# Layer-0 rows of a softmax graph network, turned by VectorE's 32x32 block transpose instead of TensorE

## The chip, the cores and the metric

One core of a Trainium2 chip runs the whole program. The metric is the device time of one execution in microseconds. The engines are TensorE (PE; its weight loads are PEld), VectorE (DVE), ScalarE (ACT) and GpSimd (POOL); SyncE (SP) issues the DMAs. Each engine runs its own list of instructions in order and meets the others at semaphores only.

## The reference

128 graphs of 64 nodes with 384 features pass through two graph networks, each followed by a residual sum and a normalisation. The change lies in the second network, two layers of this:

```python
u = jnp.einsum('bid,bjd->bij', h, h) / temper
a = jax.nn.softmax(u, axis=-1)
delta = a * adjacency_matrix
attn = delta / (jnp.sum(delta, axis=-1, keepdims=True) + 1e-10)
hl = h @ wl.T + b_l;  hs = h @ ws.T + b_s;  hr = h @ wr.T + b_r
ctx = einsum(attn * upper, hl) + diag_a[..., None] * hs + einsum(attn * lower, hr)
o = (ctx - mean) / jnp.sqrt(var + LN_EPS) * g + beta      # then relu
```

All is in float32. `h` is x1, the output of the first network, in layer 0, and the output of layer 0 in layer 1.

## The kernel before

**Tiles and units.** A unit is one layer of 512 tokens (8 graphs, `NT` = 4 tiles of 128 tokens). Two streams of 512 tokens are worked on at a time, so a pass has four units: 0 and 1 are layer 0 of stream 0 and 1, units 2 and 3 are layer 1 of them. Eight passes cover the 8192 tokens. The first network (`gated_layers`, L108 to L916) runs its eight passes first and writes x1 to DRAM; then `softmax_layers` (L919 on) runs the second. All engines' orders are written out by hand.

**High and low halves.** A float32 product is made as three products of rounded operands (`three_products`): hi x hi, hi x lo, lo x hi. ScalarE writes the high half with a copy to float32r, VectorE or GpSimd subtracts it from the full value for the low half.

**What a unit does.** Its input must lie feature-major: `ht_hi` and `ht_lo`, [128 features, 3 blocks k, 512 tokens]. In the unit before, `turn_block` (L1090) waits for the input and turns block k with four 128x128 TensorE transposes (L1104) into one of two PSUM banks `turn`; `turn_out` (L1195) on ScalarE copies the bank to `ht_hi` (L1201 in layer 0; in layer 1, L1204, gain, shift and relu as well), and `turn_lo` (L1413) on VectorE subtracts `ht_hi` from the bank into `ht_lo` (L1416). In layer 0 the input is `x_in`, rows of x1, in layer 1 it is `z`. The same banks hold the masked exponentials (`raw`, `side_prob`) until the low halves of the probabilities are made (L1454), so the first two blocks wait for `prob_lo_ready`, the third for the low half of the first.

Then come, on TensorE: `scores` (L1111, in the unit before, behind the last value), `fold_parts`, twelve `values` (L1134: 4 tiles x 3 weight matrices, nine matmuls each, into a ring of four PSUM banks) and four `contexts` (L1146: four tiles, into the same ring; tile t waits for `v_lo_ready`). VectorE empties the ring: `biased_value` (L1437) for a value, `contexts_out` (L1471) and statistics (L1474) for a context tile. ScalarE makes `v_hi` (L1238), GpSimd `v_lo` (L1329). Units of layer 1 are followed, inside the next unit, by gain and shift on GpSimd (L1353, L1355), by the residual on VectorE (L1514), by the final statistics (L1520), variance, root (L1348) and offset (L1533), and by the final normalise on ScalarE (L1244), which stands ahead of the exponentials of the unit after. So units 3 and 0 carry this extra work, and units 1 and 2 don't.

**Order around the turn (VectorE, `up_to_contexts`).** Values 3, 4, 5; probabilities; value 6; low probabilities; value 7; value 8; low halves 0 and 1; value 9; low half 2; value 10; own probability; residual (0, 1); value 11; residual (2, 3) and final statistics; contexts out; final offset. On TensorE blocks 0 and 1 are turned behind value 8 and block 2 behind value 9.

**Loads.** `load_x` (L1037) reads 512 rows of x1, row p of a tile to partition p, in pieces of 1536 bytes; SP then copies `x_in` to `x_res` for the residual (L1059), and loads `x_in` anew when the copy has landed and the blocks are turned. The very first unit of the second network is turned inside the first (`next_turn`, L393).

## Time and profile before

| | |
|---|---|
| median of 3 runs | 1760.14 us (1759.49 to 1760.24) |
| the profiled execution | 1760.6 us, span of its instructions 1758.8 us |
| TensorE matmuls | 1695.9 us busy (96% of the span), 9856 |
| VectorE | 1255.1 us (71%), 2735 |
| ScalarE | 882.7 us (50%), 1785 |
| GpSimd | 825.3 us (47%), 860 |
| second network | from about 846 us on; a pass takes 108.8 us |
| units 3, 0, 1, 2 of pass 3 and 4 | from 1275.8, 1302.7, 1330.4, 1357.3 |

A row of a timeline gives the start in us from the first instruction, the length in us of the merged run, the engine, the line of the kernel, the operation, output<-inputs with their shapes, how many instructions were merged, and in brackets the idle time of the engine before it and what ended it. Two instructions of one engine overlap by some 0.1 us in it, since the next begins while the last drains: from start to start a row of two takes less than twice one. The third number from the end of a window is the granted share of TensorE's 2.4 GHz.

### The profile page before, as it was taken

How to read it: one execution, taken by the hardware profiler on the slowest of the kernel's cores; microseconds unless marked ns; L12 is line 12 of the kernel's file. 1: busy time of each engine (PE TensorE's matmuls, PEld its weight loads, DVE VectorE, ACT ScalarE, POOL GpSimd, SP SyncE). 2: the span in 40 equal slices, each digit the busy share in tenths (PEclk: the TensorE clock that was granted, in tenths of full speed). 3: DMA queues.
4: the chain of work that ended last, by engine and by line, in shares of the span. 5: the costliest groups of instructions: out<-in, count | busy, mean ns of one | idle time of the engine just before them, and what ended most of it. 6: DMA issues, size and time to landing. Idle time of an engine off the chain costs nothing.

```text
span 1758.8 us, 30529 instructions
## 1 busy us (share of the span) xinstructions
PE 1695.9 (96%) x9856; PEld 1601.9 (91%) x9856; DVE 1255.1 (71%) x2735; ACT 882.7 (50%) x1785; POOL 825.3 (47%) x860
## 2 busy tenths in 40 slices
PE   7999999999999999999889999999999999999994
PEld 6989989898998988998789999999999999999994
DVE  4587685958768586786846867768677686776766
ACT  4545455464545546455445464454554545544542
POOL 5143242424324243334546646666465664656635
PEclk9999999999999999999899999999999999999997
DMA  7014030020202102030111020201202011020200
GB/s 224 1 31 153 6 104 15 24 89 28 91 6 64 55 24 89 6 114 17 49 50 58 21 92 21 92 0 34 80 21 92 0 54 59 21 92 0 75 1 36
DMA packets 76358, 91.98 MB, mean 52 GB/s; under 512 B 29600, under 2 KB 67488, under 8 KB 76320
## 3 DMA queue, kind: packets, MB, share of 16 engines
q1 hardware_dynamic: 76320, 91.51, 15.7%
q8 instruction: 20, 0.33, 0.1%
q14 instruction: 18, 0.15, 0.0%
HBM read 53.75 MB, written 25.17 MB: 45 GB/s over the span
## 4 chain that ended last, share of the span: by engine, by line
PE 38%; issue 36%; POOL 16%; DVE 4%; ACT 3%; SPq 1%; DMA 1%; POOLq 0%; DVEq 0%; ACTq 0%
PE b_work L1143 24%; PE b_work L1155 5%; POOL g_qv_lo L620 3%; POOL b_ht L600 3%; POOL s_v_lo L1329 3%; PE b_work L355 2%; PE b_turn L1104 2%; PE b_score_ps L105 2%; POOL b_z L1353 1%; PE b_work L379 1%; PE b_score_ps L369 1%; POOL g_keep_l L615 1%; POOL b_z L1355 1%; POOL g_sigma L629 1%; POOL g_a_nat L616 1%
## 5 line engine op out<-in xcount | busy, mean ns | idle before, releaser
L1143 PE MATMUL b_work<-b_w_hi,b_ht 128*128 128x384 f32 x2304 | 615.7, 340 | 0.0
L1143 PEld LDWEIGHTS b_work<-b_w_hi,b_ht 128*128 128x128 f32 x2304 | 420.9, 189 | 0.0
L1143 PE MATMUL b_work<-b_w_lo,b_ht 128*128 128x384 f32 x1152 | 387.4, 336 | 0.0
L355 PE MATMUL b_work<-b_ht,b_w_hi 128*128 128x512 f32 x1152 | 357.7, 392 | 9.8 <-DVE b_w_lo L695 9.8
L1329 POOL TENSOR_TENSOR s_v_lo<-s_v_full,s_v_hi 128x384 fp32r<-128x384 f32 x256 | 247.4, 983 | 198.2 <-ACT s_v_hi L1238 197.4
L620 POOL TENSOR_TENSOR g_qv_lo<-g_v_full,g_qv_hi 128x384 fp32r<-128x384 f32 x128 | 133.2, 1060 | 360.5 <-ACT g_qv_hi L493 360.5
L355 PEld LDWEIGHTS b_work<-b_ht,b_w_hi 128*128 128x128 f32 x1152 | 216.2, 189 | 51.2 <-issue 9.7
L355 PE MATMUL b_work<-b_ht,b_w_lo 128*128 128x512 f32 x576 | 225.9, 392 | 0.0
L1143 PEld LDWEIGHTS b_work<-b_w_lo,b_ht 128*128 128x128 f32 x1152 | 218.1, 189 | 0.0
L718 DVE TENSOR_TENSOR g_qv_lo<-b_work,g_qv_hi 128x512 fp32r<-128x512 f32 x192 | 128.7, 687 | 111.9 <-ACT g_qv_hi L481 110.0
L379 PE MATMUL b_work<-b_w_hi,b_ht 128*128 128x384 f32 x768 | 206.5, 336 | 0.0
L1437 DVE TENSOR_TENSOR s_v_full<-b_work,b_bias 128x384 f32<-128x384 f32 x256 | 140.3, 553 | 81.6 <-PE b_work L1143 81.6
L481 ACT ACTIVATE g_qv_hi<-b_work 128x512 fp32r<-128x512 f32 x192 | 110.6, 591 | 132.2 <-PE b_work L355 132.1
L1238 ACT ACTIVATE s_v_hi<-s_v_full 128x384 fp32r<-128x384 f32 x256 | 129.4, 529 | 86.1 <-DVE s_v_full L1437 86.1
L369 PE MATMUL b_score_ps<-g_qv_hi,b_ht 128*128 128x256 f32 x768 | 146.9, 285 | 4.8 <-DVE g_qv_lo L718 4.8
L379 PEld LDWEIGHTS b_work<-b_w_hi,b_ht 128*128 128x128 f32 x768 | 139.9, 188 | 1.3
L355 PEld LDWEIGHTS b_work<-b_ht,b_w_lo 128*128 128x128 f32 x576 | 108.7, 189 | 23.0
L379 PE MATMUL b_work<-b_w_lo,b_ht 128*128 128x384 f32 x384 | 128.8, 335 | 0.0
L369 PEld LDWEIGHTS b_score_ps<-g_qv_hi,b_ht 128*128 128x128 f32 x768 | 120.6, 188 | 8.5 <-DVE g_qv_lo L718 7.4
L1437 DVE TENSOR_TENSOR s_v_own<-b_work,b_bias 128x384 f32<-128x384 f32 x128 | 71.1, 555 | 65.3 <-PE b_work L1143 64.9
L369 PE MATMUL b_score_ps<-g_qv_lo,b_ht 128*128 128x256 f32 x384 | 107.3, 279 | 0.0
L1244 ACT ACTIVATE b_z<-b_z,s_foffset,s_frstd 128x384 f32<-128x384 f32 x62 | 39.0, 699 | 134.8 <-DVE s_foffset L1533 134.8
(138 smaller groups left out, 3225.0 us busy)
## 6 DMA issues: line engine op xcount, KB each, us to landing
b_x_in<-in_x_t SPq DMA_DIRECT2D x16, 768.0 KB, 7.0
g_x_res<-in_x SPq DMA_DIRECT2D x16, 768.0 KB, 7.7
x<-b_z SPq DMA_DIRECT2D x16, 768.0 KB, 3.9
b_x_in<-x SPq DMA_DIRECT2D x16, 768.0 KB, 5.1
s_x_res<-b_x_in SPq DMA_DIRECT2D x16, 768.0 KB, 5.4
out<-b_z SPq DMA_DIRECT2D x15, 768.0 KB, 3.6
b_a_tr<-in_adj_t SPq DMA_DIRECT2D x64, 64.0 KB, 3.4
g_a_nat<-in_adj SPq DMA_DIRECT2D x32, 64.0 KB, 2.5
```

What stands on the lines that cost most here:

```text
L355: mm = pe.matmul(bank[:], w, h, start=(n == 0), stop=(n == len(pairs) - 1))
L369: mm = pe.matmul(score_ps[:, t, :, :], h, q, start=(n == 0), stop=(n == len(pairs) - 1))
L379: mm = pe.matmul(bank[:, 0:H], h, w, start=(n == 0), stop=(n == len(pairs) - 1))
L481: nc.scalar.activation(q_hi[:, m, :, d, :], work[use % RING][:], ACT.Copy).then_inc(q_hi_ready, 1)
L600: nc.gpsimd.tensor_tensor(ht_lo[s][:, k, :], xt_in[s][:, k, :], ht_hi[s][:, k, :].bitcast(F32), ALU.subtract).then_inc(x_split, 1)
L620: nc.gpsimd.tensor_tensor(v_lo[:, t, 0:H], v_full[:, t, :], v_hi[:, t, 0:H].bitcast(F32), ALU.subtract).then_inc(v_lo_ready, 1)
L718: op = nc.vector.tensor_tensor(q_lo[:, m, :, d, :], bank, q_hi[:, m, :, d, :].bitcast(F32), ALU.subtract)
L1143: mm = pe.matmul(bank[:, 0:H], h, w, start=(n == 0), stop=(n == len(pairs) - 1))
L1155: mm = pe.matmul(bank[:, 0:HC], p, v, start=(n == 0), stop=(n == len(pairs) - 1))
L1238: nc.scalar.activation(v_hi[:, t, n, 0:H], v_full[:, (2 * t + n) % VF, :], ACT.Copy)\
L1329: nc.gpsimd.tensor_tensor(v_lo[:, t, n, 0:H], v_full[:, (2 * t + n) % VF, :], v_hi[:, t, n, 0:H].bitcast(F32), ALU.subtract).then_inc(v_lo ...
L1437: nc.vector.tensor_tensor(dst, work[(unit * WN + j) % RING][:, 0:H], bias[:, side, layer, :], ALU.add).then_inc(work_free, 1)
```

## The change

Layer-0 rows of the second network are no longer turned by TensorE, except for the very first unit.

- `load_x` reads x1 in four DMAs, one for each quarter of 32 partitions. Partition q*32+t of block b (16 blocks of 32 tokens) holds token b*32+t, features q*96 to q*96+95: pieces of 384 bytes.
- `flip_block` on VectorE turns block k with one instruction over [128, 16 x 32]: 32 features of every third column, 32x32 blocks, into `turned_x`, a new SBUF buffer of two slots [128, 2, 512]. It waits for the load, and for k = 2 for the low half of block 0. Row p of block k is now feature 3p + k, so the layer-0 weights are loaded in that order too, and `next_turn` reads every third column.
- `turn_out` and `turn_lo` of layer 0 read `turned_x` in place of the PSUM bank.
- Order: on VectorE the flips 0 and 1 stand behind values 3 and 4, ahead of the probabilities; low half 0 and flip 2 behind value 7; low half 1 behind value 8; low half 2 behind value 9. On ScalarE blocks 0 and 1 stand ahead of `values_hi(2)`.
- `x_res` is read from x1 in DRAM, no longer copied from `x_in`, and SP no longer waits for that copy.

```diff
             def load_x(i, s):
-                sp.dma_start(x_in[s][:], x_v[i, s]).then_inc(x_loaded[s], 16)
+                for q in range(QUADS):
+                    sp.dma_start(sh.x_blocks[s][quarter(q)], x_b[i, s, q]).then_inc(x_loaded[s], 16)
...
-                    sp.wait_ge(x_loaded[s], 16 * (i + 1))
-
                     wait(sp, summed, i * (STREAMS * NT) + (s + 1 - STREAMS) * NT)
-                    sp.dma_start(x_res[s][:], x_in[s][:]).then_inc(x_copied[s], 16)
+                    sp.dma_start(x_res[s][:], x_v[i, s]).then_inc(x_copied[s], 16)
                     if not last:
                         sp.wait_ge(turned, nth(i, s, KO, KO - 1))
-                        sp.wait_ge(x_copied[s], 16 * (i + 1))
                         load_x(i + 1, s)
...
+                    turn_next = more and layer_of(unit + 1) == 1
...
-                    if more:
+                    if turn_next:
                         turn_block(i, unit + 1, 0)
                         turn_block(i, unit + 1, 1)
...
                 if layer == 0:
-                    nc.scalar.activation(ht_hi[s][:, k, :], bank[:], ACT.Copy).then_inc(turn_read, 1)
+                    nc.scalar.activation(ht_hi[s][:, k, :], turned_x[:, k % XK, :], ACT.Copy).then_inc(turn_read, 1)
...
+                flip_next = more and layer_of(unit + 1) == 0
+                if flip_next:
+                    turn_out(i, unit + 1, 0)
+                    turn_out(i, unit + 1, 1)
                 values_hi(i, unit, 2)
...
             def turn_lo(i, unit, k):
                 s = unit % STREAMS
+                full = turned_x[:, k % XK, :] if layer_of(unit) == 0 else turn[(unit * KO + k) % 2][:]
                 dve.wait_ge(turn_read, nth(i, unit, KO, k))
-                nc.vector.tensor_tensor(ht_lo[s][:, k, :], turn[(unit * KO + k) % 2][:],
-                                        ht_hi[s][:, k, :].bitcast(F32), ALU.subtract).then_inc(ht_ready, 1)
+                nc.vector.tensor_tensor(ht_lo[s][:, k, :], full, ht_hi[s][:, k, :].bitcast(F32),
+                                        ALU.subtract).then_inc(ht_ready, 1)
+
+            def flip_block(i, unit, k):
+                s = unit % STREAMS
+                dve.wait_ge(x_loaded[s], x_parts(i, unit))
+                if k >= XK:
+                    dve.wait_ge(ht_ready, nth(i, unit, KO, k - XK))
+                blocks = sh.x_blocks[s][:, :, k:KO * QUAD:KO]
+                nc.vector.transpose(turned_x[:, k % XK, :].rearrange("p (b t) -> p b t", b=TOK // QUAD), blocks)\
+                    .then_inc(turned, 1)
...
                 for j in range(3, 6):
                     biased_value(i, unit, j)
+                    if flip_next and j - 3 < XK:
+                        flip_block(i, unit + 1, j - 3)
                 probabilities(i, unit)
                 biased_value(i, unit, 6)
                 probabilities_lo(i, unit)
                 biased_value(i, unit, 7)
+                if flip_next:
+                    turn_lo(i, unit + 1, 0)
+                    flip_block(i, unit + 1, 2)
                 biased_value(i, unit, 8)
                 if more:
-                    turn_lo(i, unit + 1, 0)
+                    turn_lo(i, unit + 1, 1 if flip_next else 0)
+                if turn_next:
                     turn_lo(i, unit + 1, 1)
```

At the start of the second network the written-out order gets the same: flips 0, 1, 2 behind values 3, 4, 5, low half 0 behind value 5, low half 1 behind value 7, low half 2 behind value 9 as before.


## Rows read from the trace of the kernel before

**Rows 1.** Waits, second network: who waited for whom, us, times, longest.

```profile
PE b_turn L1104 <- DVE b_ht L1416: 16.8, 17, 7.1
...
PE b_work L1155 <- POOL s_v_lo L1329: 5.5, 7, 0.8
```

**Rows 2.** Timeline of TensorE, unit 0: start, us, engine, line, op [idle before <-releaser].

```profile
1317.46 1.04 PE L1104 MATMUL b_turn<-b_const,b_x_in 128*128 128x128 f32 x8
...
1323.51 1.59 PE L105 MATMUL b_score_ps<-b_ht 128*128 128x256 f32 x12
...
1329.26 0.44 PE L1155 MATMUL b_work<-s_v_hi,s_prob_hi 128*128 128x386 f32 x1 [0.79 <-POOL s_v_lo L1329]
```

**Rows 3.** Timeline of VectorE, unit 0, a value at TensorE's pace.

```profile
1311.41 0.56 DVE L1437 TENSOR_TENSOR s_v_full<-b_work,b_bias 128x384 f32<-128x384 f32 x1 [1.00 <-PE b_work L1143]
```

**Rows 4.** Timelines of ScalarE (first two) and GpSimd, unit 0.

```profile
1306.98 2.51 ACT L1244 ACTIVATE b_z<-b_z,s_foffset,s_frstd 128x384 f32<-128x384 f32 x4 [7.55 <-DVE s_foffset L1533]
...
1311.01 0.96 ACT L1238 ACTIVATE s_v_hi<-s_v_full 128x384 fp32r<-128x384 f32 x2
...
1311.64 1.85 POOL L1329 TENSOR_TENSOR s_v_lo<-s_v_full,s_v_hi 128x384 fp32r<-128x384 f32 x2 [2.80 <-ACT s_v_hi L1238]
...
1324.54 4.59 POOL L1329 TENSOR_TENSOR s_v_lo<-s_v_full,s_v_hi 128x384 fp32r<-128x384 f32 x4
```

**Rows 5.** Timeline of VectorE, unit 3 and the start of unit 0.

```profile
1289.87 0.55 DVE L1437 TENSOR_TENSOR s_v_full<-b_work,b_bias 128x384 f32<-128x384 f32 x1
...
1293.76 0.56 DVE L1437 TENSOR_TENSOR s_v_full<-b_work,b_bias 128x384 f32<-128x384 f32 x1 [0.18 <-PE b_work L1143]
...
1294.74 0.69 DVE L1416 TENSOR_TENSOR b_ht<-b_turn,b_ht 128x512 fp32r<-128x512 f32 x1 [0.42 <-ACT b_ht L1201]
...
1295.76 0.56 DVE L1437 TENSOR_TENSOR s_v_full<-b_work,b_bias 128x384 f32<-128x384 f32 x1 [0.33 <-PE b_work L1143]
...
1296.83 1.70 DVE L1514 SCALAR_TENSOR_TENSOR b_z<-b_z,s_x_res 128x384 f32<-128x384 f32 x2
...
1306.80 0.15 DVE L1533 SCALAR_TENSOR_TENSOR s_foffset<-s_fmv,s_frstd 128x4 f32<-128x4 f32 x1
```

**Rows 6.** One line's instructions (duration ns min/median/max): reduce from SBUF; L1416.

```profile
L1459 DVE TENSOR_REDUCE s_own<-s_expo x32: 674/676/678, 879.1 to 1730.1; 128x4 f32<-128x512 f32 x32
...
L1416 DVE TENSOR_TENSOR b_ht<-b_turn,b_ht x93: 676/692/694, 873.8 to 1703.9; 128x512 fp32r<-128x512 f32 x93
```

**Rows 7.** L706's instructions; timelines of VectorE beside GpSimd; GpSimd alone (last row).

```profile
L706 DVE TENSOR_TENSOR b_ht<-g_ht_full,b_ht x48: 691/693/1336, 53.8 to 811.9; 128x512 fp32r<-128x512 f32 x48
...
809.26 1.16 DVE L706 TENSOR_TENSOR b_ht<-g_ht_full,b_ht 128x512 fp32r<-128x512 f32 x1 [2.76 <-ACT b_ht L473]
...
810.81 2.46 DVE L706 TENSOR_TENSOR b_ht<-g_ht_full,b_ht 128x512 fp32r<-128x512 f32 x2
...
806.91 7.24 POOL L606 TENSOR_TENSOR b_w_lo<-g_next_stage,b_w_hi 128x384 fp32r<-128x384 f32 x6 [9.09 <-ACT b_w_hi L456]
...
900.35 5.82 POOL L1313 TENSOR_TENSOR b_w_lo<-s_x_res,b_w_hi 128x384 fp32r<-128x384 f32 x6 [2.34 <-ACT b_w_hi L1193]
```

**Rows 8.** Timeline of GpSimd, unit 3.

```profile
1293.55 2.81 POOL L1329 TENSOR_TENSOR s_v_lo<-s_v_full,s_v_hi 128x384 fp32r<-128x384 f32 x3
```

**Rows 9.** Windows: stretch, busy of each engine, granted clock, DMA share, GB/s.

```profile
843.60:845.90 2.30, 0.00 (x1) 0.01 (x1) 1.23 (x4) 1.01 (x2) 2.05 (x3) 1.00 0.13 29
...
846.30:849.70 3.40, 3.40 (x16) 3.40 (x16) 0.93 (x3) 0.93 (x3) 2.98 (x3) 0.50 0.00 0
```

**Rows 10.** Timelines at the start: TensorE (first two), VectorE.

```profile
874.58 1.11 PE L1104 MATMUL b_turn<-b_const,b_x_in 128*128 128x128 f32 x4 [6.17 <-DVE b_ht L1416]
...
880.89 1.59 PE L105 MATMUL b_score_ps<-b_ht 128*128 128x256 f32 x12
...
876.36 0.69 DVE L1416 TENSOR_TENSOR b_ht<-b_turn,b_ht 128x512 fp32r<-128x512 f32 x1 [0.27 <-ACT b_ht L1201]
```

**Rows 11.** SP's loads of x rows: issue ns min/median/max.

```profile
L1038 SPq DMA_DIRECT2D b_x_in<-x x14: 363/398/403, 924.0 to 1567.8; - x14
```

More of the change, by code:

```diff
@@ L21 @@
 BIG = 1e30
+QUAD = 32
+QUADS = P // QUAD
 C_EYE, C_LE, C_GT, C_LT = 0, 128, 256, 384
@@ L69, in __init__ @@
         self.x_in = [sb(f"x_in{s}", [P, NT, H]) for s in range(STREAMS)]
+        self.x_blocks = [b[:].rearrange("p t h -> p (t h)").rearrange("p (b f) -> p b f", b=TOK // QUAD)
+                         for b in self.x_in]
         self.a_tr = [sb(f"a_tr{s}", [P, NT, P]) for s in range(STREAMS)]
@@ L91, in __init__, with quarter @@
         self.adj_loaded = [ctx.enter_context(nc.semaphore(f"b_adj_loaded{s}")) for s in range(STREAMS)]
+def quarter(q):
+    return slice(q * QUAD, (q + 1) * QUAD)
 def three_products(H_hi, H_lo, W_hi, W_lo):
@@ L280, in one_pass @@
                         sp.wait_ge(stored[s], 16 * 2)
-                        sp.dma_start(x_in[s][:], x1_v[0, s]).then_inc(sh.x_loaded[s], 16)
+                        if s == 0:
+                            sp.dma_start(x_in[s][:], x1_v[0, s]).then_inc(sh.x_loaded[s], 16)
+                        else:
+                            for q in range(QUADS):
+                                sp.dma_start(sh.x_blocks[s][quarter(q)], x1_b[0, s, q]).then_inc(sh.x_loaded[s], 16)
                 for s in range(STREAMS):
@@ L298, in next_weights @@
             def next_weights(n):
[L299 removed]
+                sp.dma_start(next_stage[n % 2][:], next_w[n][0].rearrange("(p k) o -> p k o", p=P))\
                     .then_inc(next_stage_in[n], 16)
@@ L400, in next_turn @@
                 for t in range(NT):
-                    mm = pe.transpose(turn[k % 2][:, t * P:(t + 1) * P], x_in[0][:, t, k * P:(k + 1) * P], eye)
+                    mm = pe.transpose(turn[k % 2][:, t * P:(t + 1) * P], x_in[0][:, t, k:H:KO], eye)
                 mm.then_inc(sh.turned, 1)
@@ L935, in softmax_layers @@
     LAST_GT = 1
+    XK = 2
     VF = 4
@@ L959, in softmax_layers @@
         expo = sb("expo", [P, NT, P])
+        turned_x = sb("turned_x", [P, XK, TOK])
         prob_hi = [sb(f"prob_hi{n}", [P, NT, P], F32R) for n in range(2)]
@@ L1020, in layer_of, with x_parts @@
             return unit % UNITS // STREAMS
+        def x_parts(i, unit):
+            s = unit % STREAMS
+            return 16 * QUADS * (i + unit // UNITS + s) + 16 * (1 - s)
         def in_layer(i, unit):
@@ L1037, in load_x @@
             def load_x(i, s):
-                sp.dma_start(x_in[s][:], x_v[i, s]).then_inc(x_loaded[s], 16)
+                for q in range(QUADS):
+                    sp.dma_start(sh.x_blocks[s][quarter(q)], x_b[i, s, q]).then_inc(x_loaded[s], 16)
             def load_adj(i, s):
@@ L1090, in turn_block @@
             def turn_block(i, unit, k):
-                layer, s = divmod(unit % UNITS, STREAMS)
-                src = x_in[s] if layer == 0 else z[s]
-                if layer == 0:
-                    pe.wait_ge(x_loaded[s], i * 16 + 16 * (unit // UNITS + 1))
-                else:
-                    pe.wait_ge(z_ready, i * (STREAMS * NT) + NT * (s + 1))
+                s = unit % STREAMS
+                pe.wait_ge(z_ready, i * (STREAMS * NT) + NT * (s + 1))
                 if k < 2:
@@ L1103, in turn_block @@
                 for t in range(NT):
-                    mm = pe.transpose(bank[:, t * P:(t + 1) * P], src[:, t, k * P:(k + 1) * P], eye)
+                    mm = pe.transpose(bank[:, t * P:(t + 1) * P], z[s][:, t, k * P:(k + 1) * P], eye)
                 mm.then_inc(turned, 1)
@@ L1171, in one_pass @@
                     values(i, unit, 9)
-                    if more:
+                    if turn_next:
                         turn_block(i, unit + 1, 2)
@@ L1268, in second_half @@
                 if more:
-                    for k in range(KO):
+                    for k in range(2 if flip_next else 0, KO):
                         turn_out(i, unit + 1, k)
@@ L1293, in _ @@
             gated_normalise(0)
-            for t in range(3):
-                values_hi(0, 0, t)
-            for k in range(KO):
-                turn_out(0, 1, k)
+            values_hi(0, 0, 0)
+            values_hi(0, 0, 1)
+            turn_out(0, 1, 0)
+            turn_out(0, 1, 1)
+            turn_out(0, 1, 2)
+            values_hi(0, 0, 2)
             values_hi(0, 0, 3)
@@ L1545, in up_to_contexts @@
                 more = not (last and unit == UNITS - 1)
+                flip_next = more and layer_of(unit + 1) == 0
+                turn_next = more and layer_of(unit + 1) == 1
                 for j in range(3, 6):
                     biased_value(i, unit, j)
+                    if flip_next and j - 3 < XK:
+                        flip_block(i, unit + 1, j - 3)
                 probabilities(i, unit)
@@ L1605, in _ @@
             biased_value(0, 0, 3)
+            flip_block(0, 1, 0)
             gated.gain_and_shift(2)
             biased_value(0, 0, 4)
+            flip_block(0, 1, 1)
             gated.gain_and_shift(3)
             biased_value(0, 0, 5)
+            turn_lo(0, 1, 0)
+            flip_block(0, 1, 2)
             gated.residual_and_stats((0, 1))
@@ L1612, in _ @@
             biased_value(0, 0, 7)
+            turn_lo(0, 1, 1)
             gated.residual_and_stats((2, 3))
             biased_value(0, 0, 8)
-            turn_lo(0, 1, 0)
-            turn_lo(0, 1, 1)
             gated.final_var()
```

5 lines of the change are left out of this document (4 added, 1 removed).

## The prediction

> **What bounds the kernel now.** I read the page first: TensorE is busy 96% of the span, VectorE 71%, GpSimd 47%. So 12 transposes less per layer-0 unit ought to be time won, and the question is where something else ends last. The waits of the second network answer it [rows 1]: TensorE waits for VectorE's low halves at the third transpose, mostly in two start-up stalls, and 7 times, 0.8 us each, for GpSimd's low halves of the values (L1329). That second wait stands once per pass, in unit 0, and unit 0 comes right after unit 3. These are the two units that turn the layer-0 rows of a next unit. Units 1 and 2 turn z, which the change leaves alone; there TensorE runs through.
>
> Then the timeline of these two units. TensorE's first transpose in unit 0 is at 1317.46 and the scores at 1323.51 [rows 2]; the 27 matmuls between take 3 x 1.56 us (one value per 0.56 busy and 1.00 idle on VectorE [rows 3]), so 12 transposes cost 6.05 - 4.68 = 1.37 us. In the same rows the last context tile starts at 1329.26, after 0.79 us of idle TensorE. What comes before it is a chain through four engines [rows 4]: the final offset on VectorE (1306.80), ScalarE's final normalise that waited 7.55 us for it and behind which the exponentials and the first v_hi stand, GpSimd's first v_lo at 1311.64, which waited 2.80 us for that v_hi, and then GpSimd without a pause until the four v_lo from 1324.54 have ended at 1329.13. The offset in turn ends an unbroken run of VectorE that begins with the value of 1295.76 in unit 3 [rows 5], which waited 0.33 us for TensorE. So unit 0 ends when this chain lets it, and only the part of the gain that moves the chain's start counts there.
>
> **TensorE.** 15 units lose 1.37 us of transposes: 7 times in unit 3, 7 times in unit 0, once at the start. Taken alone, 20.6 us. In unit 0 this is covered by the wait for GpSimd, which is there already: 7 x 1.37 us worth nothing, unless GpSimd's chain gets shorter. What is left to win is unit 3's share, if it arrives at 1295.76.
>
> **VectorE in unit 3.** Added: three flips. The trace has no block transpose; the nearest row is the reduce over 128x512 from SBUF, 0.68 us, or 0.59 from start to start [rows 6]. I take 0.60; bounds 0.5 and 1.3 (twice the reduce). The first two stand behind values 3 and 4, where VectorE idles a microsecond or more per value, and are hidden. The third lies in the tight stretch. The three low halves (L1416) move from bank + SBUF to two SBUF inputs, turned_x and ht_hi. The same subtraction with two SBUF inputs is L706: 693 ns in the median, but 1.16 and 2 x 1.23 us in the three that run beside GpSimd's L606 [rows 7], so 1.16 us from start to start against 0.61. In unit 3 GpSimd is at work in this stretch too [rows 8]. After value 7 VectorE is free at 1290.34: low half 1.16, flip 0.60, value 8 0.47, low half 1.16, value 9 0.47, low half 1.16 give 1295.36 for value 10, against 1295.76 now [rows 5]. Of TensorE's 1.37 us some 0.4 arrive. The residual adds of 1296.83, also with two SBUF inputs, then run beside a GpSimd that is later, for which I take off 0.2. The chain starts 0.2 us earlier. Bounds: 1.37 earlier (no contention), 0.6 later (slow flip). TensorE's scores wait for the third low half at 1295.4 and are not due before 1295.9: hidden.
>
> **GpSimd in unit 0.** Six subtractions of one form take 5.82 us alone and 7.24 us beside those three low halves [rows 7]: (7.24 - 5.82) / 3 = 0.47 us lost to GpSimd per contended low half. In unit 0 the three low halves fall on the unbroken run of rows 4: 3 x 0.47 = 1.4 us later at its end. Bounds 0.9 (0.3 each) and 2.1 (each holds GpSimd for its 0.69). With one SBUF input, as L1416 has now, they cost nothing: its 93 stay within 676 to 694 ns. The Trainium skill has a rule for this, in "SBUF — State Buffer", section "SBUF: two separate sides": VectorE with two SBUF inputs and GpSimd exclude each other for a whole instruction. Rows 7 agree in kind; by the rule the loss would be the upper bound, an estimate of 5 us more in all.
>
> Sum for a pass: 1.4 - 0.2 = 1.2 us later, times 7 = 8.4 us.
>
> **The clock.** TensorE now comes to the wait of unit 0 earlier by 2 x 1.37 us less some 0.6 (value 0 of unit 0 must wait for its bank, freed by a VectorE that didn't gain). The third context tile needs v_lo from the middle of the last GpSimd group, some 1.2 us later than now, so 2.1 + 1.2 = 3.3 us open up in front of it, less what VectorE's late low halves take of it at the scores: 2.5 to 3.3 us of idle, and about 1 us more stands in front of the fourth. When TensorE was idle for 2.35 us at 843.5 (0.00 busy in that window), 3.4 us at a granted clock of 0.50 followed [rows 9], that is the lower level, 1.2 GHz. 3.4 us at half speed cost 1.7, less 0.3 that fall on the idle: 1.4. The idle is about as long as the one row that I have, so I count half of the passes: 7 x 0.5 x 1.4 = 4.9 us.
>
> **The start.** TensorE's stall of 6.17 us before 874.58 and the half speed behind it go; what is late next is the third low half, which the scores wait for. It starts at 876.36 and would be 3 flips (1.8) and up to 1.5 us of contention later, so it ends between 878.8 and 880.3, against scores at 880.89 [rows 10]. A gain of 0.5 to 2; I take 1.5. The other start-up stall (7.1 us [rows 1]) stands in unit 1, which turns z, and stays.
>
> **What costs nothing.** Four loads for one on SP's queue, 0.40 us of issue each [rows 11], and pieces of 384 B for 1536: issued two units (some 50 us) before their use, where even four times the present 5.0 us to land is hidden; behind them on SP stand only adjacency loads and output stores. x_res is read from DRAM at the same point of the queue, and SP loses two waits. ScalarE turns blocks 0 and 1 ahead of values_hi(2): 1.2 us later for GpSimd, which is behind anyway in these units. The flips' own waits hold nobody: the rows have long landed, and the third follows on VectorE right behind the low half that it waits for. The strided read of 12 transposes at the start is 3 us of TensorE at most beside a VectorE that bounds.
>
> **Sum**, on the profiled execution (1760.6 us; span 1758.8 and 1.8 around it; 0.03% above the median of 1760.14): 1760.6 + 8.4 + 4.9 - 1.5 = 1772 us.
>
> **Rivals.**
> 1. *The low halves do not collide.* They could fall between GpSimd's instructions. Then value 10 starts 1.37 us earlier, GpSimd's chain too, and no long idle appears: 1760.6 - 7 x 1.37 - 2 = 1749 us. Against it: both engines are busy without pause there, and all three L706 beside L606 were hit. Chance 0.18.
> 2. *Break-even.* 0.9 us lost on GpSimd, 0.9 won at value 10, no clock loss: 1759 us. Chance 0.17.
> 3. *A slow flip.* The source is read at a stride of 12 bytes. At 1.3 us each the third flip delays value 10 by 0.7 in each of 7 passes, and the start by up to 2: about 1778 us. No row speaks for it or against. The Trainium skill, "Advanced Engine Details and Errata", section "SBUF Cachelines", wants at least two accesses per 16-byte line, which this stride gives only every third time; no run here shows it. Chance 0.13.
> 4. *The loads come too late*, so that flips wait: excluded by the 50 us, 0.02.
>
> The forecast itself, the collision in unit 0 outweighing unit 3's gain: 0.50. It turns into a gain where the loss on GpSimd falls under what reaches value 10. Slower side: with the clock falling in every pass and 2.1 us on GpSimd, 1782. Range 1754 to 1784; it leaves out most of rival 1. A measurement can tell about 0.2% (3.5 us) from no change. Faster takes rival 1 and a part of 2: 0.22; same the rest of 2: 0.15; slower 0.63.
>
> **What would show it.** Right: L1104 left with the transposes of z alone; the low halves at 1.0 to 1.3 us instead of 0.69 in units 3 and 0; GpSimd's unbroken run in unit 0 longer by 1.4 us than 17.5; TensorE's wait for v_lo at 3 us and more per pass, and stretches at 0.50 clock near it; flips at 0.6. Wrong: low halves at 0.69, or TensorE without a wait in unit 0, or passes of the second network that get shorter.

## The result and the profile after

The changed kernel takes 1772.57 us in the median of 4 runs (1772.5 to 1772.76), the kernel before on the same chip 1760.19 us (1759.49 to 1760.44): the ratio is 1.0071, with a 95% interval of 1.0054 to 1.0089. It is slower by 12.4 us. The profiled execution took 1772.5 us, its span is 1770.7 us against 1758.8.

In the changed kernel the lines have other numbers: values L1159, contexts L1171, the fold that opens a unit L1136, the scores L114, the low halves L1440, the flips L1450, the residual adds L1548, the context tiles on VectorE L1505, GpSimd's v_lo L1352, gain and shift L1376 and L1378.

Waits of TensorE after the change (us in total, times, longest), the answer to [rows 1]:

```profile
PE b_work L1171 <- POOL s_v_lo L1352: 16.0, 14, 1.5
PE b_turn L1120 <- DVE b_ht L1440: 10.8, 16, 7.2
...
PE b_score_ps L114 <- DVE b_ht L1440: 6.6, 8, 0.9
PE b_work L1159 <- DVE b_z L1505: 5.4, 7, 0.8
...
PE b_work L1159 <- DVE s_v_full L1471: 3.7, 2, 2.8
...
PE b_work L1159 <- DVE s_v_own L1471: 2.1, 1, 2.1
```

One start-up stall has gone. The wait for GpSimd's low halves has grown from 5.5 us in 7 to 16.0 us in 14, and four kinds of wait are new. Where they stand shows TensorE's timeline of one unit 0 (start, us, op [idle before <- releaser]), the answer to [rows 2]:

```profile
1307.81 0.40 PE L1136 MATMUL b_score_ps<-b_part,b_eye_r 128*128 128x256 f32 x2
...
1309.38 0.44 PE L1159 MATMUL b_work<-b_w_hi,b_ht 128*128 128x384 f32 x1 [0.78 <-DVE b_z L1505]
...
1329.22 1.69 PE L114 MATMUL b_score_ps<-b_ht 128*128 128x256 f32 x12 [0.85 <-DVE b_ht L1440]
...
1334.56 0.44 PE L1171 MATMUL b_work<-s_v_hi,s_prob_hi 128*128 128x386 f32 x1 [1.53 <-POOL s_v_lo L1352]
1336.66 0.44 PE L1171 MATMUL b_work<-s_v_hi,s_prob_hi 128*128 128x386 f32 x1 [0.80 <-POOL s_v_lo L1352]
1337.83 0.40 PE L1136 MATMUL b_score_ps<-b_part,b_eye_r 128*128 128x256 f32 x2
```

Four waits, 3.96 us, between the fold of unit 0 and that of unit 1. A unit is measured here from fold to fold: this one is 1337.83 - 1307.81 = 30.02 us long. The same subtraction gives, in us, for a pass in which the clock stays up:

| kernel | unit 2 | unit 3 | unit 0 | unit 1 | a pass |
|---|---|---|---|---|---|
| before | 27.35 | 26.88 | 27.71 | 26.86 | 108.8 |
| after | 27.35 | 25.56 | 30.02 | 26.88 | 109.8 |

Unit 3 gained 1.32 us, unit 0 lost 2.31. Times 7 that is 6.9 us. In 2 of the 7 passes the granted clock fell behind these waits as well, and units 0 and 1 were together 1.6 us longer than in the others: 3.2 us. Up to unit 2 of the first pass 2.0 us were lost. The sum is 12.1 us, against 11.9 us of span.

VectorE and GpSimd in the same unit 0 (VectorE's three low halves; GpSimd from the start to the end of its run, answering [rows 4]):

```profile
1323.74 1.49 DVE L1440 TENSOR_TENSOR b_ht<-s_turned_x,b_ht 128x512 fp32r<-128x512 f32 x1
...
1326.56 1.19 DVE L1440 TENSOR_TENSOR b_ht<-s_turned_x,b_ht 128x512 fp32r<-128x512 f32 x1
...
1328.14 1.03 DVE L1440 TENSOR_TENSOR b_ht<-s_turned_x,b_ht 128x512 fp32r<-128x512 f32 x1
```

```profile
1318.01 1.85 POOL L1352 TENSOR_TENSOR s_v_lo<-s_v_full,s_v_hi 128x384 fp32r<-128x384 f32 x2 [2.91 <-ACT s_v_hi L1255]
...
1323.66 2.29 POOL L1352 TENSOR_TENSOR s_v_lo<-s_v_full,s_v_hi 128x384 fp32r<-128x384 f32 x2
1325.91 1.29 POOL L1363 TENSOR_TENSOR s_expo<-s_expo,s_keep 128x512 f32<-128x512 f32 x1
1327.17 1.46 POOL L1376 TENSOR_TENSOR b_z<-b_z,b_gain 128x384 f32<-128x384 f32 x1
1328.70 1.34 POOL L1378 TENSOR_TENSOR b_z<-b_z,b_shift 128x384 f32<-128x384 f32 x1
...
1331.97 4.56 POOL L1352 TENSOR_TENSOR s_v_lo<-s_v_full,s_v_hi 128x384 fp32r<-128x384 f32 x4
```

Each low half lengthens the GpSimd operation that comes next: 2.29 us against the 1.85 of the same pair at 1318.01, 1.46 and 1.34 against 1.02 each for gain and shift left alone. And the low halves are long themselves, in a way that shows what happens. The second one ends at 1326.56 + 1.19 = 1327.75, and the GpSimd operation that was at work when it began ended at 1325.91 + 1.29 = 1327.20, 0.55 us earlier. That distance is 0.55 us in all 43 low halves that began beside a GpSimd operation, whether 0.33 or 0.94 us of that operation were left. The GpSimd operation behind it ends 0.72 or 0.87 us after the low half (42 of the 43; such an operation takes 0.87 or 1.02 us alone). So the two engines take turns, operation by operation: VectorE waits for the end of GpSimd's, and GpSimd's next then waits for VectorE, all but its first 0.15 us. The two kinds of L1440 in the whole run, and the flips (duration ns min/median/max):

```profile
L1440 DVE TENSOR_TENSOR b_ht<-b_turn,b_ht x48: 690/691/694, 911.3 to 1715.8; 128x512 fp32r<-128x512 f32 x48
L1440 DVE TENSOR_TENSOR b_ht<-s_turned_x,b_ht x45: 675/998/1486, 869.4 to 1659.1; 128x512 fp32r<-128x512 f32 x45
...
L1450 DVE STREAM_TRANSPOSE s_turned_x<-b_x_in x45: 851/877/895, 862.3 to 1656.2; 128x512 f32<-128x512 f32 x45
```

One line, one shape, one output; the one operand that comes from the PSUM bank instead of SBUF goes with the difference between 694 and 1486 ns at most. The 48 from the bank stand in other units, where GpSimd works less beside them; but in the kernel before, 28 of the 93 low halves [rows 6] had GpSimd at work for over nine tenths of their length, and took 680 to 692 ns. The flips stay within 44 ns of each other, whatever GpSimd does.

### The profile page after: what moved, and what is told of

It reads as the page before. It is cut to its first block, busy times and chain, and to the rows that moved or that the text cites. A ratio compares the mean times of both kernels' runs of the same rounds, so it can differ in the third digit from the quotient of the medians.

```text
span 1770.7 us, 30284 instructions
## 1 busy us (share of the span) xinstructions
PE 1685.3 (95%) x9676; PEld 1587.0 (90%) x9676; DVE 1313.4 (74%) x2780; ACT 884.0 (50%) x1785; POOL 842.4 (48%) x860
## 4 chain that ended last, share of the span: by engine, by line
issue 44%; POOL 24%; PE 21%; DVE 6%; ACT 3%; SPq 1%; DMA 1%; POOLq 1%; DVEq 0%; ACTq 0%
PE b_work L1159 11%; POOL s_v_lo L1352 6%; POOL g_qv_lo L634 3%; POOL b_ht L614 3%; POOL b_z L1376 2%; PE b_work L1171 2%; PE b_work L369 2%; POOL b_z L1378 2%; PE b_work L393 1%; PE b_score_ps L383 1%; POOL s_expo L1363 1%; POOL s_keep L1346 1%; POOL g_keep_l L629 1%; POOL g_sigma L643 1%; POOL g_a_nat L630 1%
## 5 line engine op out<-in xcount | busy, mean ns | idle before, releaser
L1159 PE MATMUL b_work<-b_w_hi,b_ht 128*128 128x384 f32 x2304 | 610.6, 340 | 11.2 <-DVE b_z L1505 5.4
L1159 PEld LDWEIGHTS b_work<-b_w_hi,b_ht 128*128 128x128 f32 x2304 | 421.7, 190 | 13.3 <-DVE b_z L1505 6.4
L1159 PE MATMUL b_work<-b_w_lo,b_ht 128*128 128x384 f32 x1152 | 387.7, 337 | 0.0
L1352 POOL TENSOR_TENSOR s_v_lo<-s_v_full,s_v_hi 128x384 fp32r<-128x384 f32 x256 | 255.5, 1015 | 200.9 <-ACT s_v_hi L1255 199.9
L1159 PEld LDWEIGHTS b_work<-b_w_lo,b_ht 128*128 128x128 f32 x1152 | 218.6, 190 | 0.0
```

The costliest lines, as they stand in the source:

```text
L1159: mm = pe.matmul(bank[:, 0:H], h, w, start=(n == 0), stop=(n == len(pairs) - 1))
L1352: nc.gpsimd.tensor_tensor(v_lo[:, t, n, 0:H], v_full[:, (2 * t + n) % VF, :], v_hi[:, t, n, 0:H].bitcast(F32), ALU.subtract).then_inc(v_lo ...
```

## The experiments

Twelve kernels, each against the kernel before on the same chip. All of them are about three questions: is it the collision, why does the saved TensorE time not arrive without it, and what holds the units then.

### 1. The collision and the flips, each alone

The changed kernel, low halves from the bank:

```diff
-                full = turned_x[:, k % XK, :] if layer_of(unit) == 0 else turn[(unit * KO + k) % 2][:]
+                full = turn[(unit * KO + k) % 2][:]
...
-                                        ALU.subtract).then_inc(ht_ready, 1)
+                                        ALU.is_equal if layer_of(unit) == 0 else ALU.subtract).then_inc(ht_ready, 1)
```

> The changed kernel, but the low halves of layer 0 take their first input from the PSUM bank again instead of turned_x (and compare instead of subtracting, so that the numbers stay small: ht_lo of layer 0 is then no low half, and the output is another). Flips, loads, orders stay as changed. Theory (two SBUF inputs collide with GpSimd): low halves at 0.69 us; GpSimd's unbroken run in unit 0 back from 18.5 to 17.5 us; the run starts 1.0 to 1.4 us earlier after the start of unit 3 than before the change; a pass is 1.2 to 1.4 us shorter than before, so 1751 to 1753 us. Rival (the flips, of 0.88 us each, or the new orders are what costs): no more than 2 us below the changed kernel's 1772.6.

Measured: 1760.95 us, ratio 1.0004 (0.9994 to 1.0014). The 12 us are back, but no more than that: the 1751 to 1753 us expected are missed by 8.

The kernel before, low halves of layer 0 from SBUF (a buffer that is set to zero once):

```diff
+                full = turned_x[:, k % 2, :] if layer_of(unit) == 0 else turn[(unit * KO + k) % 2][:]
...
-                nc.vector.tensor_tensor(ht_lo[s][:, k, :], turn[(unit * KO + k) % 2][:],
+                nc.vector.tensor_tensor(ht_lo[s][:, k, :], full,
```

> The kernel before, transposes on TensorE and all, with one edit: the low halves of layer 0 read a buffer of zeros in SBUF in place of the PSUM bank (ht_lo is then no low half, and the output is another). Theory: low halves at 0.9 to 1.5 us, GpSimd's run in unit 0 1.0 to 1.4 us longer, TensorE's wait for v_lo as much longer, 7 passes: 1767 to 1770 us. Rival (SBUF input is harmless there, the flips or the loads cost): 1760 to 1761 us.

Measured: 1775.97 us, ratio 1.0096 (1.0079 to 1.0112): more than the whole loss and 6 us above the range expected, with TensorE's transposes still in place and no flip anywhere. Its unit 0 is 29.4 us, and in one pass the clock falls as well. Its low halves of layer 0 (L1419 here) lengthened as in the change:

```profile
L1419 DVE TENSOR_TENSOR b_ht<-s_turned_x,b_ht x45: 678/1039/1773, 874.7 to 1660.7; 128x512 fp32r<-128x512 f32 x45
```

The kernel before with flips into a buffer that nobody reads, behind values 3, 4 and 7. There are 42 of them and not the 45 of the expectation, since the start of the second network has none:

```diff
                 for j in range(3, 6):
                     biased_value(i, unit, j)
+                    if flip_next and j < 5:
+                        flip_block(i, unit + 1, j - 3)
...
                 biased_value(i, unit, 7)
+                if flip_next:
+                    flip_block(i, unit + 1, 2)
```

> The kernel before, with 45 block transposes added on VectorE at the places of the change, into a buffer that nobody reads; TensorE still turns. The source is read in the old layout, at the same stride of 12 bytes. Theory: a flip has one SBUF input and doesn't hold GpSimd; the first two fit where VectorE waits for TensorE, the third into 2.2 us of idle time in unit 3: 1760 to 1763 us, the start of the second network taking what there is. Rival (a slow flip is the cause): 1766 us or more.

Measured: 1760.28 us, ratio 1.0 (0.9991 to 1.001). The flips of the passes fall into VectorE's idle time; those at the start were not tested alone.

So the loss is the collision. It was shown both ways: put in alone it costs 16 us, taken out it gives 12 back. The kernel that gives them back has the new loads and orders too, so these are not what costs. A form of the change that keeps all its work and reads the bank: ScalarE copies the turned block a second time, into the bank, and its copies and the low halves stand in the order of before.

```diff
-                    nc.scalar.activation(ht_hi[s][:, k, :], turned_x[:, k % XK, :], ACT.Copy).then_inc(turn_read, 1)
+                    nc.scalar.activation(ht_hi[s][:, k, :], turned_x[:, k % XK, :], ACT.Copy)
...
+                    nc.scalar.activation(bank[:], turned_x[:, k % XK, :], ACT.Copy).then_inc(turn_read, 1)
```

> A repair: ScalarE copies each turned block from turned_x to ht_hi and then also into the PSUM bank, once the bank is free, and the low half reads the bank, in the order of before (halves 0 and 1 behind value 8, half 2 behind value 9); flip 2 stands behind low half 0. Three more ScalarE copies of 0.6 us for each layer-0 unit, at a place where ScalarE idles. Theory: no contention, TensorE's saving in unit 3 reaches GpSimd's run: 1751 to 1754 us, faster than both. Rival: ScalarE's second copy makes the low halves late, TensorE waits at the scores, and the time is between 1756 and 1765.

Measured: 1764.87 us, ratio 1.0025 (1.0015 to 1.0034). Better than the change by 7.7 us, but not the 1751 to 1754 expected. It lies in the range of its rival, and the rival is right in part: TensorE waits 0.48 us at the scores of unit 0. But it also waits 0.52 and 1.11 us for v_lo there. Both kernels without the collision miss their expectation by about 10 us, so something else stands in unit 0.

### 2. Why the saving does not arrive: GpSimd's run

TensorE in a unit 0 of the first kernel above (low halves from the bank):

```profile
1435.39 0.44 PE L1171 MATMUL b_work<-s_v_hi,s_prob_hi 128*128 128x386 f32 x1 [1.73 <-POOL s_v_lo L1352]
1437.19 0.44 PE L1171 MATMUL b_work<-s_v_hi,s_prob_hi 128*128 128x386 f32 x1 [0.47 <-POOL s_v_lo L1352]
```

Units 3 and 0 are 25.55 and 28.3 us, together 53.85 against 54.59 before: of 2 x 1.37 us saved 0.74 arrive. The rest has turned into the wait for v_lo. And the clock takes back what arrives. In four of the seven passes it stays up, and a pass is 108.1 us, 0.7 less than before. In the other three it falls to half for 3.4 to 6.8 us, which makes them 1.5 to 2.9 us longer, 6.0 us in all, more than the 7 x 0.74 = 5.2 us that arrive; the kernel before has no such stretch in a pass. So this kernel is level with the kernel before, and not some 5 us faster, because of the clock.

GpSimd's run, from its first v_lo to its last in unit 0, starts 35.26 us after unit 3's start here and 35.83 before. VectorE explains why the start is only 0.57 us earlier; value 10 and the adds behind it, in unit 3 of this kernel:

```profile
1403.10 0.56 DVE L1471 TENSOR_TENSOR s_v_full<-b_work,b_bias 128x384 f32<-128x384 f32 x1 [0.33 <-PE b_work L1159]
...
1404.16 2.49 DVE L1548 SCALAR_TENSOR_TENSOR b_z<-b_z,s_x_res 128x384 f32<-128x384 f32 x2
```

Value 10 is 1.3 us earlier (18.61 us into the unit against 19.95), but the residual adds, two SBUF operands as well, now meet GpSimd's v_lo and take 2.49 us against 1.70 [rows 5].

Two experiments on that run. First, the changed kernel with GpSimd's last gain and shift of a pass over 8 columns:

```diff
+                w = 8 if s == 1 and t == 3 else H
...
-                nc.gpsimd.tensor_tensor(z[s][:, t, 0:H], z[s][:, t, 0:H], gain[:], ALU.mult).then_inc(gained, 1)
+                nc.gpsimd.tensor_tensor(z[s][:, t, 0:w], z[s][:, t, 0:w], gain[:, 0:w], ALU.mult).then_inc(gained, 1)
...
```

> The changed kernel, with GpSimd's last gain and shift of each pass (unit 3, tile 3, 0.86 and 1.06 us) over 8 columns instead of 384, so the output isn't the reference's there: GpSimd's run is some 1.7 us shorter and nothing else is changed. Theory (GpSimd's run ends unit 0): 1.5 to 1.8 us less a pass and the clock drops with it, 1758 us (1756 to 1762). Rival (VectorE's lengthened low halves end it, and GpSimd only seems to be waited for): over 1769 us.

Measured: 1759.61 us, ratio 0.9997 (0.9987 to 1.0006): 13 us less than the changed kernel, for 1.24 us less work on GpSimd in a pass. The two operations of that run:

```profile
1325.34 0.19 POOL L1377 TENSOR_TENSOR b_z<-b_z,b_gain 128x8 f32<-128x8 f32 x1
1325.62 0.49 POOL L1379 TENSOR_TENSOR b_z<-b_z,b_shift 128x8 f32<-128x8 f32 x1
```

0.68 us against 0.86 + 1.06 in the changed kernel. Unit 0 is 28.82 us, 1.2 less, and no half-clock stretch is left in the passes. GpSimd's run ends unit 0; with the collision untouched, shortening it pays one for one: 7 x 1.2 us and the 3.2 us of the clock are 11.6 of the 13.

Second, an order that starts the run earlier. ScalarE idles 7.55 us ahead of block 0's last normalising [rows 4]; that goes behind the normalise of unit 3:

```diff
                     normalise(i, unit, more)
+                    if unit == UNITS - 1 and not last:
+                        final_normalise(i, 0)
...
-                    if unit >= STREAMS:
+                    if unit == UNITS - 1 or last and unit == STREAMS:
                         final_normalise(i, unit - STREAMS, tiles=NT if more else NT // 2)
```

On the kernel before:

> The kernel before, with one thing moved: in unit 3 ScalarE's normalising of the finished block 0 (2.5 us, which waits for VectorE's offset) goes from ahead of unit 0's exponentials and v_hi 0 to behind the normalise. All work is done. Theory (GpSimd's run of 17.5 us, which v_hi 0 releases 35.8 us after unit 3's start, is what ends unit 0, and ScalarE stands idle for 7.5 us ahead of it): the run starts some 2.8 us earlier, TensorE's wait of 0.8 us for v_lo in each of 7 passes goes, 1754.5 us (1753 to 1756). Rival (that wait is something else's, or GpSimd's earlier halves collide with VectorE and give it back): 1760 us.

On the changed kernel:

> The changed kernel with the same one thing moved (block 0's normalising on ScalarE goes behind unit 3's normalise). The low halves still read two SBUF operands beside GpSimd. Theory (the collisions cost time only because they lengthen GpSimd's run and VectorE's chain, which end unit 0): unit 0 falls from 30.0 us to about 27.2 us (25.5 of TensorE's own work and the waits of 0.78 and 0.85 us for a value bank and a low half), 1750 us (1748 to 1754). Rival (VectorE's collisions hold TensorE by themselves): under 5 us gained, above 1767 us.

On the variant with the copies into the bank:

> The kernel in which ScalarE also copies the turned block into the PSUM bank and the low half reads the bank (1764.9 us), with the same normalising moved. Theory: its unit 0 waits 0.5 and 1.1 us for GpSimd's low halves, both go, unit 0 falls from 28.5 to about 26.9 us, its unit 1 of 27.8 us stays: 1753 us (1751 to 1756). Rival: no better than 1763 us.

Measured, in this order: 1759.78 us (ratio 0.9996, 0.9987 to 1.0005), 1768.65 us (1.0046, 1.003 to 1.0061) and 1757.6 us (0.9984, 0.9975 to 0.9993). The first two miss and fall on the rival's side, the third is 1.6 us above its range. The run does start earlier. The wait for GpSimd is gone from unit 0 in the first and third kernel and down to 0.46 us in the second. But the time comes back in unit 1 (passes in which the clock stays up):

| kernel | unit 3 | unit 0 | unit 1 | a pass |
|---|---|---|---|---|
| before | 26.88 | 27.71 | 26.86 | 108.8 |
| before, reordered | 26.88 | 26.60 | 27.85 | 108.7 |
| after | 25.56 | 30.02 | 26.88 | 109.8 |
| after, reordered | 25.55 | 27.82 | 28.91 | 109.6 |
| low halves from the bank | 25.55 | 28.31 | 26.88 | 108.1 |
| copies into the bank | 25.55 | 28.54 | 27.81 | 109.3 |
| the same, reordered | 25.55 | 26.77 | 28.44 | 108.1 |

### 3. The second chain: VectorE

Rows of the reordered kernel before: GpSimd's run (its first and last group), TensorE at the start of unit 1, and VectorE ahead of it.

```profile
1308.87 1.85 POOL L1331 TENSOR_TENSOR s_v_lo<-s_v_full,s_v_hi 128x384 fp32r<-128x384 f32 x2
...
1322.22 4.27 POOL L1331 TENSOR_TENSOR s_v_lo<-s_v_full,s_v_hi 128x384 fp32r<-128x384 f32 x4
```

```profile
1329.29 0.40 PE L1120 MATMUL b_score_ps<-b_part,b_eye_r 128*128 128x256 f32 x2
1330.61 0.44 PE L1143 MATMUL b_work<-b_w_hi,b_ht 128*128 128x384 f32 x1 [0.52 <-DVE b_z L1473]
```

```profile
1322.34 0.56 DVE L1439 TENSOR_TENSOR s_v_full<-b_work,b_bias 128x384 f32<-128x384 f32 x1 [0.34 <-PE b_work L1143]
...
1323.41 2.35 DVE L1516 SCALAR_TENSOR_TENSOR b_z<-b_z,s_x_res 128x384 f32<-128x384 f32 x2
...
1326.15 1.22 DVE L1516 SCALAR_TENSOR_TENSOR b_z<-b_z,s_x_res 128x384 f32<-128x384 f32 x2
1327.29 1.93 DVE L1522 BATCH_NORM_STATS2 s_fstats<-b_z 128x6 f32<-128x384 f32 x4
...
1329.94 0.62 DVE L1473 SCALAR_TENSOR_TENSOR b_z<-s_v_own,s_own,b_work 128x385 f32<-128x385 f32 x1
```

GpSimd's run starts at 1308.87 instead of 1311.64 and ends at 1326.49 instead of 1329.13 (the two unit 3 start within 0.01 us of each other). VectorE gains nothing from it: from value 10, at TensorE's pace, over the adds and the final statistics to the first context tile it is busy without a pause for 8 us, and that tile is taken out of its bank at 1329.94. Value 0 of unit 1 needs the bank. In the kernel before the same tile is taken out at nearly the same time (VectorE), and value 0 of unit 1 (TensorE) finds its bank free:

```profile
1330.00 0.62 DVE L1471 SCALAR_TENSOR_TENSOR b_z<-s_v_own,s_own,b_work 128x385 f32<-128x385 f32 x1
```

```profile
1331.06 0.39 PE L1143 MATMUL b_work<-b_w_hi,b_ht 128*128 128x384 f32 x1
```

The bank is free at 1330.00 + 0.62 = 1330.62. So TensorE came only 0.44 us too late to wait for this chain; where it comes earlier, because the wait for GpSimd is gone, the chain holds it.

I tried to take the second by order too: the first two context tiles ahead of the final statistics, GpSimd's masks ahead of its final root.

```diff
                     add_residual(i, s, (2, 3))
+                    contexts_out(i, unit, (0, 1))
                     final_stats(i, s)
                     final_var(i, s)
-                contexts_out(i, unit)
-                if s is not None:
+                    contexts_out(i, unit, (2, 3))
                     final_offset(i, s)
+                else:
+                    contexts_out(i, unit)
```

On the reordered variant with the copies, on the reordered kernel before, and on the kernel with low halves from the bank, in this order:

> The bank variant with the normalising moved (1757.6 us), and VectorE's own chain shortened too: in units 3 and 0 the first two context tiles are taken out of their banks ahead of the final statistics (2.5 us) instead of behind them, and GpSimd's masks go ahead of its final root. All work is done. Theory (two chains end units 0 and 1: GpSimd's run, and VectorE's from value 10 over the residual adds and the statistics to the context tiles whose banks value 0 of the next unit takes): TensorE's waits of 0.4 and 1.1 us for those banks go, the wait of 0.8 for a low half stays; 1747.5 us (1745 to 1751). Rival (VectorE only shifts its work, and the later tiles or the next unit's values are late in their place): 1755 us or more.

> The kernel before with both moves (the normalising on ScalarE, the context tiles on VectorE and the masks on GpSimd), no block transposes. With the first alone unit 0 was 1.1 us shorter and unit 1 1.0 us longer (1759.8 us). Theory: that unit 1's wait of 0.5 us and what goes with it is VectorE's chain, and goes now: unit 1 back at 26.86, 1.1 us less a pass, 1752.5 us (1751 to 1755). Rival (it is something else's): 1759 us or more.

> The changed kernel, its low halves reading the PSUM bank (a compare with whatever is in it, so the low half of layer 0 is left out), and both moves. It shows what taking the transposes off TensorE is worth once neither chain holds the units. Theory: units 0 and 3 are TensorE's own 25.5 us each, 105.3 us a pass against 108.8: 24 us less, 1736 us (1734 to 1741). Rival (something else holds unit 0 above 26.5 us): 1744 us or more.

Measured: 1763.59 us (ratio 1.002, 1.0011 to 1.0029), 1765.42 us (1.003, 1.0019 to 1.0041) and 1752.03 us (0.9953, 0.9939 to 0.9967). All three came out on the rival's side, the third 16 us above its expectation. VectorE and TensorE in the second of them:

```profile
1328.12 2.31 DVE L1516 SCALAR_TENSOR_TENSOR b_z<-b_z,s_x_res 128x384 f32<-128x384 f32 x2
1330.36 0.60 DVE L1473 SCALAR_TENSOR_TENSOR b_z<-s_v_own,s_own,b_work 128x385 f32<-128x385 f32 x1
...
1335.13 0.62 DVE L1473 SCALAR_TENSOR_TENSOR b_z<-s_v_own,s_own,b_work 128x385 f32<-128x385 f32 x1
```

```profile
1331.27 0.40 PE L1120 MATMUL b_score_ps<-b_part,b_eye_r 128*128 128x256 f32 x2
1335.80 0.44 PE L1143 MATMUL b_work<-b_w_hi,b_ht 128*128 128x384 f32 x1 [0.55 <-DVE b_z L1473]
```

The wait has moved from the first bank to the third, whose tile stands behind the statistics now, and the masks, moved forward, meet the second pair of adds (2.31 us against 1.22). In all three kernels TensorE now waits another 0.7 us in unit 1, for the low probabilities. Unit 1 became 28.6 to 29.3 us in the three. This order only shifted a chain in which VectorE never idles. So the last kernel leaves work out: low halves from the bank, ScalarE's order moved, context tiles in their old place, the final statistics over 8 columns.

```diff
-                    nc.vector.bn_stats(fstats[:, t, :], z[s][:, t, 0:H]).then_inc(fstats_ready, 1)
+                    nc.vector.bn_stats(fstats[:, t, :], z[s][:, t, 0:8]).then_inc(fstats_ready, 1)
```

> The changed kernel with its low halves reading the PSUM bank (layer 0's low half left out), the normalising of block 0 moved on ScalarE, the context tiles in their old place, and VectorE's final statistics over 8 columns instead of 384 (so the last normalisation's mean and variance are of 8 columns): both chains shortened, one by order and one by leaving 1.4 us of work out. Theory (GpSimd's run and VectorE's chain from value 10 to the context tiles are what keeps TensorE's saving from arriving): unit 0 about 25.8 us and unit 1 26.9 us, 105.7 us a pass against 108.8, 1739 us (1736 to 1743). Rival (a third thing holds the units, as unit 1's 28.6 us in the last run may say): 1748 us or more.

Measured: 1729.7 us, ratio 0.9829 (0.9813 to 0.9846), 9 us below even the 1739 expected. A pass is 27.35 + 25.55 + 25.10 + 26.90 = 104.9 us. Three of the four waits of TensorE that are left in the second network:

```profile
PE b_turn L1120 <- DVE b_ht L1442: 10.8, 16, 7.1
...
PE b_work L1159 <- DVE s_v_full L1473: 3.6, 2, 2.5
...
PE b_score_ps L114 <- DVE b_ht L1442: 0.2, 1, 0.2
```

No wait for GpSimd's v_lo (L1354) and none for a bank taken out by a context tile (b_z) is in the list. Unit 0 is 27.71 - 25.10 = 2.6 us shorter than before: its 1.37 us of transposes, its 0.79 us of wait, and 0.45 us that a stop and a restart cost beside. TensorE's saving arrives in full, in unit 0 as in unit 3, once neither chain holds the units. The price is 1.57 us of VectorE's work in each of them (the statistics take 0.36 us instead of 1.93), which a kernel that does all the work has to place elsewhere. Not all of the 30 us is the transposes': they are 7 x 2 x 1.37 = 19 us, and the wait and the restart of unit 0 are 8.7; most of what is left is the first network, 1.7 us shorter in this execution. No run has VectorE's chain shortened alone, or both chains shortened with the transposes on TensorE.

Of the kernels that do all the work, the one with copies into the bank and ScalarE's order moved is the fastest: 1757.6 us, 15 us less than the change and 2.6 us less than before.

## Why the prediction was right

The forecast was 1772 us and its mechanism is that of the runs: the collision in unit 0 outweighs unit 3's gain, through GpSimd's run. That the sum came within 0.6 us is luck in part, two errors that cancel: the start was 3.5 us worse than forecast, the passes and the clock together 3.2 us better.

- **What bounds.** Right, and shown by the kernel with the short gain and shift. Incomplete: the prediction followed one chain back from the wait that the profile names. VectorE's chain into unit 1 had no wait in any list, since TensorE came to its bank 0.44 us after it was free.
- **TensorE's 1.37 us.** Right: unit 3 is 1.32 us shorter. That unit 0's share is covered is right too: it arrived only where both chains were shortened.
- **The flip.** 0.60 us was taken, 0.80 us from start to start (877 ns) was measured, within the bounds of 0.5 and 1.3. The rival of a slow flip is out; and with an idle VectorE around two of three it would have cost little (the flips alone: 1760.28 us).
- **Low halves in unit 3.** 1.16 us from start to start was taken from the rows of the first network; here they last 0.99, 0.91 and 0.88 us. Value 10 starts 18.95 us into unit 3 against 19.95, so 1.0 us earlier and not 0.4:

```profile
1301.20 0.55 DVE L1471 TENSOR_TENSOR s_v_full<-b_work,b_bias 128x384 f32<-128x384 f32 x1
...
1302.26 2.43 DVE L1548 SCALAR_TENSOR_TENSOR b_z<-b_z,s_x_res 128x384 f32<-128x384 f32 x2
...
1305.08 1.22 DVE L1548 SCALAR_TENSOR_TENSOR b_z<-b_z,s_x_res 128x384 f32<-128x384 f32 x2
...
1313.17 0.14 DVE L1567 SCALAR_TENSOR_TENSOR s_foffset<-s_fmv,s_frstd 128x4 f32<-128x4 f32 x1
```

- **The residual adds.** The term that was sized worst: 0.2 us was taken off for them. The first pair alone costs 0.73 us more (2.43 against 1.70 [rows 5]), and the offset at the end of the run comes 30.92 us into the unit against 30.99. The chain starts 0.07 us earlier, not 0.2. An operation that already had two SBUF operands and ran just behind GpSimd's work was moved into it by the very time that was won.
- **GpSimd's run in unit 0.** 18.52 us (1318.01 to 1336.53) against 17.49: 1.03 us more where 1.4 was forecast. The three low halves cost it 0.44 + 0.44 + 0.32 = 1.2 us, 0.40 each against 0.47; some 0.2 come back, as the GpSimd operations behind them take that much less than in the kernel before. The Trainium skill ("SBUF — State Buffer", section "SBUF: two separate sides") states that a VectorE instruction with two SBUF inputs and a GpSimd instruction that reads SBUF exclude each other for the whole instruction. The trace agrees, in kind and in time: the 0.55 us between the end of GpSimd's operation and that of the low half is the same 43 times. What the prediction made of the rule, 0.69 us lost to GpSimd for each low half, was too much. GpSimd's next operation begins beside the low half and has its first 0.15 us done, and where 0.08 us would have lain between the two anyway that is saved as well, so 0.44 or 0.32 us are lost. VectorE itself loses 0.2 to 0.8 us (0.88 to 1.49 against 0.69), where the prediction took half a microsecond throughout.
- **A pass.** Forecast 1.2 us, measured 1.0.
- **The clock.** Forecast in half of the passes at 1.4 us, 4.9 in all; it came in 2 of 7 at 1.6 us, 3.2 in all, and once more at the start for 1.1 us, where none was forecast. The idle was not one piece of 2.5 to 3.3 us but 0.85, 1.53 and 0.80 us, and TensorE's wait for v_lo 2.3 us in a pass where "3 us and more" was to show it. Windows of one of the two (stretch, busy of each engine, granted clock):

```profile
1444.00:1446.50 2.50, 1.40 (x7) 1.09 (x7) 2.46 (x5) 0.00 (x0) 2.30 (x3) 1.00 0.00 0
...
1446.90:1450.20 3.30, 3.30 (x14) 3.29 (x14) 3.08 (x7) 0.00 (x0) 3.05 (x3) 0.50 0.00 0
```

- **The start.** Forecast a gain of 1.5 us; it is a loss of 2.0. The step looked at the scores alone and asked whether the third low half would be ready. But VectorE also frees the banks of the values, and its first flips and low halves now stand ahead of them:

```profile
869.53 0.44 PE L1159 MATMUL b_work<-b_w_hi,b_ht 128*128 128x384 f32 x1 [2.06 <-DVE s_v_own L1471]
...
875.23 0.69 PE L1159 MATMUL b_work<-b_w_hi,b_ht 128*128 128x384 f32 x1 [2.81 <-DVE s_v_full L1471]
...
881.68 1.70 PE L114 MATMUL b_score_ps<-b_ht 128*128 128x256 f32 x12 [0.78 <-DVE b_ht L1440]
```

  One stall of 6.17 us became four of 0.88, 2.06, 2.81 and 0.78 us, with the clock at half for 10.2 us around them instead of 6.8. Unit 0 of the first pass is 36.08 us against 35.50. With the low halves from the bank it is 35.49, so these 0.6 us are the collision; without it the gain is still nought, because the waits for the value banks stay (3.5 and 2.1 us in that kernel). Unit 1 is 36.51 us against 35.42, and this is the clock: behind its stall of 7.2 us, which is nearly that of before (7.1), the clock stays at half for 10.2 us instead of 6.8. The collision does not decide that. Unit 1 is 36.5 us with 10.2 us at half in the kernel with the flips alone, and 35.2 us with 6.8 in the kernel with the collision alone. The last 0.3 of the 2.0 us lie ahead of the second network's first fold.
- **What costs nothing.** Right: no wait of TensorE or VectorE for the loads is in the trace, though a quarter of the rows takes 6.6 us to land.

```profile
b_x_in<-x SPq DMA_DIRECT2D x60, 192.0 KB, 6.6
```

- **Rivals.** "The low halves do not collide" would have given 1749 us. The kernel in which they don't gave 1761, so this price was 12 us too low. It let value 10's 1.37 us reach GpSimd's chain, where the adds take half of it: a pass gains 0.7 us, not 1.37, 4.6 us in all. It expected no idle long enough for the clock, but there are 1.73 us in each unit 0 and 3 stretches at half speed, 6.0 us. And it counted on 2 us at the start, where none came.

What stays open: why the same waits lower the clock in two passes and not in the other five, why the second start-up stall is followed by 10.2 us at half speed in some kernels and 6.8 in others, and how much of the flip's 877 ns is its stride of 12 bytes, which no run varied.

## What to carry to other kernels

When work leaves the busiest engine, look for every chain that ends within a microsecond of the wait you see, also those that have no wait yet: here two did, and shortening GpSimd's alone gave nothing (1759.8 us against 1760.2). Before an operand is moved from PSUM to SBUF on VectorE, ask whether GpSimd works beside it: the same subtraction went from 0.69 to 1.0 us in the median and slowed GpSimd by 0.4 us each time, and one extra copy on ScalarE, which had idle time, was cheaper by 7.7 us. Time won on a chain moves what stands behind it, and it may be moved into a collision, as the residual adds were. Read the clock before you judge a kernel that gained nothing: the one without the collision had gained 5 us and lost 6 to half speed.

## What the hardware showed

- The block transpose of 128x512 float32 takes 851 to 895 ns and did not collide: 858 ns in the mean where GpSimd was idle (7 of 45), 878 ns where it was at work for over nine tenths of the time (36). It has one SBUF input and an SBUF output. The subtraction with one SBUF and one PSUM input, and an SBUF output too, stays within 676 to 694 ns in the kernel before.
- Two SBUF inputs on VectorE beside GpSimd: 1.08 us in the mean, 0.88 to 1.49, in the 43 low halves of 45 that began beside a GpSimd operation. Each ended 0.55 us after that operation; the residual adds that met one, with 384 columns, ended 0.41 to 0.42 us after it (51 of 64).
- On GpSimd a multiplication over 8 columns takes 0.19 to 0.22 us, one over 384 columns 0.86 to 1.02 alone.
